# Routing from centred raw tokens in the mixtures of a macaron kernel

## The reference

```
x = x + 0.5 * ffn(layernorm(x))          # F0: two layers of local attention and gated MLP
x = x + ssm(layernorm(x))                # S
x = x + 0.5 * ffn(layernorm(x))          # F1
x = x + 0.5 * mixture(layernorm(x))      # M0
x = x + unit(layernorm(x))               # U: RMS norm, two projections, silu, product, output
x = x + 0.5 * mixture(layernorm(x))      # M1

def mixture(x):                          # 8 experts, top 2, hidden 512
    probs = softmax(x @ w_router)
    topk_w, topk_idx = top_k(probs, 2)   # weights are not renormalised over the two
    out_e = gelu(x @ w1[e] + b1[e]) @ w2[e] + b2[e]
    return sum over the chosen e of topk_w * out_e
```

## Time and profile before

| | us |
|---|---|
| median of 3 runs | 1197.33 (1192.86 to 1198.54) |
| profiled execution | 1189.11, span 1187.3 |
| PE busy | 1012.3 (85%) |
| DVE busy | 720.2 (61%) |
| ACT busy | 688.2 (58%) |
| POOL busy | 524.8 (44%) |
| mean granted TensorE clock | 0.926 |

### The profile page before, as it was taken

The page is one execution under the profiler, slowest core; times in us unless marked ns, Lnnn a source line. Parts: engine busy times, 40 slices in busy tenths (PEclk is TensorE's granted clock), DMA queues, the critical chain, the costliest instruction groups (busy, mean ns, idle before and its releaser), DMA issues.

```text
span 1187.3 us, 25908 instructions
## 1 busy us (share of the span) xinstructions
PE 1012.3 (85%) x9070; PEld 632.4 (53%) x9070; DVE 720.2 (61%) x1625; ACT 688.2 (58%) x1301; POOL 524.8 (44%) x405
## 2 busy tenths in 40 slices
PE   4788999999998876799999999999639968746995
PEld 1345555555555364355555555555339964325995
DVE  0577678777776653677776776876564423654441
ACT  2566686686673662676677667656316636623661
POOL 2664456556441542545444344433345530263451
PEclk9899999999999967999999999999759989857997
DMA  9895344455433600545444344432312240011223
GB/s 349 250 298 157 86 102 109 97 120 116 100 93 81 71 1 2 126 109 121 96 107 96 89 107 109 101 80 77 143 44 68 67 114 1 19 43 48 64 65 120
DMA packets 88511, 120.02 MB, mean 101 GB/s; under 512 B 20064, under 2 KB 72032, under 8 KB 87488
## 3 DMA queue, kind: packets, MB, share of 16 engines
q1 hardware_dynamic: 81824, 96.30, 33.8%
q0 software_dynamic: 6272, 20.44, 4.7%
q10 hardware_dynamic: 288, 1.63, 0.3%
HBM read 62.66 MB, written 22.11 MB: 71 GB/s over the span
## 4 chain that ended last, share of the span: by engine, by line
PE 65%; ACT 14%; issue 7%; DMA 6%; DVE 5%; POOL 1%; SPq 1%; ACTq 0%; DVEq 0%; POOLq 0%
PE banks L591 7%; PE banks L944 6%; PE banks L954 6%; PE banks L676 5%; PE banks L662 5%; PE banks L620 3%; PE banks L751 3%; PE banks L669 3%; PE banks L637 3%; PE banks L721 3%; PE banks L726 2%; PE banks L645 2%; DMA rstd<-arena 2%; ACT arena L1194 2%; ACT arena L1189 2%
## 5 line engine op out<-in xcount | busy, mean ns | idle before, releaser
L2041 POOL TENSOR_TENSOR arena<-arena 128x1024 f32<-128x1024 f32 x64 | 150.9, 2357 | 321.0 <-DVE arena L1644 318.7
L2030 POOL TENSOR_TENSOR arena<-arena 128x1024 f32<-128x1024 f32 x64 | 150.8, 2357 | 41.6 <-ACT arena L1189 41.6
L1636 DVE TENSOR_REDUCE arena<-banks 128x4 f32<-128x512 f32 x128 | 82.5, 686 | 93.5 <-PE banks L620 93.3
L1181 ACT ACTIVATE arena<-banks,arena 128x512 f32<-128x512 f32 x128 | 80.5, 679 | 93.6 <-PE banks L669 93.2
L591 PE MATMUL banks<-arena 128*128 128x512 f32 x256 | 128.6, 627 | 6.7 <-DVE arena L1563 5.9
L2020 POOL DMA_INDIRECT moe_outs<-arena x78 | 81.5, 1045 | 100.7 <-DVE arena L1882 88.6
L1386 ACT ACTIVATE arena<-banks,arena 128x128 f32<-128x128 f32 x312 | 89.0, 369 | 59.0 <-PE banks L944 58.9
L2013 POOL DMA_INDIRECT moe_rows<-arena x64 | 63.1, 986 | 118.5 <-DVE arena L1617 101.1
L1644 DVE TENSOR_TENSOR arena<-arena 128x1024 f32<-128x1024 f32 x64 | 78.1, 1220 | 28.4 <-DMA arena<-arena 28.4
L1194 ACT ACTIVATE arena<-banks 128x1024 f32<-128x1024 f32 x64 | 65.6, 1025 | 46.1 <-PE banks L591 45.1
L954 PE MATMUL banks<-arena 128*128 x624 | 87.5, 283 | 4.6 <-ACT arena L1386 4.4
(11 more groups left out here) (221 smaller groups left out, 1951.6 us busy)
## 6 DMA issues: line engine op xcount, KB each, us to landing
arena<-arena SPq DMA_DIRECT2D x256, 128.0 KB, 3.8
arena<-rstd SPq DMA_DIRECT2D x128, 256.0 KB, 4.3
moe_rows<-arena POOLq DMA_DIRECT2D x12, 903.0 KB, 6.6
arena<-moe_rows SPq DMA_DIRECT2D x78, 64.5 KB
arena<-in_rot SPq DMA_DIRECT2D x4, 1024.0 KB, 11.6
arena<-in_mw SPq DMA_DIRECT2D x2, 2048.0 KB, 10.8
arena<-moe_outs SPq DMA_DIRECT2D x16, 256.0 KB, 4.9
arena<-ssm_a SPq DMA_DIRECT2D x4, 512.0 KB, 6.6
```

The costliest lines, as they stand in the source:

```text
L1636: nc.vector.tensor_reduce(mx[:, e], by_row(bank[3 + e][:]), AX.X, ALU.max).then_inc(s_max, 1)
L2030: nc.gpsimd.tensor_tensor(TA[:, n % 2], RAW, ROTV[:, :, 0, c * C:(c + 1) * C], ALU.mult).then_inc(cos_done, 1)
L2041: nc.gpsimd.tensor_tensor(TA[:, n % 2], TA[:, n % 2], TB, ALU.add).then_inc(rot_sum, 1)
```

## The change

The mixture's norm no longer works on features as partitions. At the start of F1 the router matrix is multiplied with `centre` once (`centred_router`), and logits are raw: X times the centred router. VectorE picks the top two from these raw logits (`pick`, 5 steps, reading the accumulator). Tokens come out centred and transposed by one matmul with `centre` on the right (`token_rows`). VectorE takes the variance of each token with bn_stats and bn_aggr (`moments`), ScalarE makes the inverse roots, four columns a chunk, and scales the tokens while it copies them. The softmax weights (`gates_start`, `gates_exp`, `gates_end`) are computed once for all 16 tiles, behind the tile map. `rank` and the scatter are as before. In F1's tail chunks 1 and 2 are handled earlier; in the unit, `down(0)` and `added(0)` come before chunk 3 of M0 is combined, and each chunk of M1 enters by one step `enter`.

```diff
-        MX_CEN, MX_VAR = [(0, 3, 7, 3), (7, 7, 7, 7)], [(1, 4, 6, 5), (3, 4, 5, 3)]
+        MX_TOK, MX_RANK = [(0, 3, 3, 7), (7, 7, 3, 7)], [(1, 4, 4, 6), (3, 4, 5, 4)]
 # SP: ins["mwr"] -> WR is loaded behind WM[1] at the start, no longer at M0
 # TensorE
+            def centred_router():
+                pe.wait_ge(wrc, 16)
+                mm(bank[7][:, 0:NE], centre, WR, start=True, stop=True).then_inc(wrc, 1)
+            def route(moe, c):
+                pe.wait_ge(wrc, 18)
+                for t in range(TILES):
+                    at = c * C + t * P
+                    last = mm(bank[MX_RANK[moe][c]][:, t * NE:(t + 1) * NE], X[:, at:at + P], WRC, start=True, stop=True)
+                last.then_inc(router_mm, 1)
+            def token_rows(moe, c):
+                for t in range(TILES):
+                    at = c * C + t * P
+                    last = mm(bank[MX_TOK[moe][c]][:, t * P:(t + 1) * P], X[:, at:at + P], centre, start=True, stop=True)
+                last.then_inc(xtok_mm, 1)
 # TensorE, ffn tail (run 1): token_rows(0, 0) for centred, route(0, 0) for variance; then
-                    pe.wait_ge(xtok_done, 2)
+                    pe.wait_ge(xtok_done, 1)
                 transpose_out(30, n - 2, s, 0)
                 for e in range(2):
                     values(31, n - 1, e)
                 if run:
                     pe.wait_ge(x_ffn, NCH + 2)
-                    centred(X, 1, MX_CEN[0][1])
+                    token_rows(0, 1)
+                    route(0, 1)
...
                 last_variance()
                 if run:
-                    variance(mix, 1, MX_VAR[0][1])
+                    rank(0, 1)
                 mlp_output(6, s)
                 last_hidden(0)
                 last_hidden(1)
-                if run:
-                    route(mix, 0, 1)
                 last_hidden(2)
+                if run:
+                    pe.wait_ge(xtok_done, 3)
+                    pe.wait_ge(rank_dve, 2 * RANK_STEPS)
+                    pe.wait_ge(x_ffn, NCH + 3)
+                    token_rows(0, 2)
+                    route(0, 2)
                 mlp_output(7, s)
 # TensorE, start of mixture 0: rank(0, 2); token_rows(0, 3); route(0, 3); rank(0, 3)
 # TensorE, unit, order after: mixed(2) up(0) centred(2) down(0) mixed(3) up(1) enter(0) variance(2)
 #   centred(3) down(1) rank(0) variance(3) enter(1) up(2, 0..2) rank(1) up(2, 3) up(3)
 #   down(2) down(3) enter(2) rank(2) enter(3) rank(3)
+                def enter(c):
+                    pe.wait_ge(x_unit, c + 1)
+                    if c == 2:
+                        pe.wait_ge(rank_dve, RANK_STEPS * (NCH + 1))
+                    elif c:
+                        pe.wait_ge(xtok_done, 2 * NCH + (1 if c == 1 else 3))
+                    token_rows(1, c)
+                    if c in (1, 2):
+                        pe.wait_ge(sn_out, SN0 + c + 2)
+                    elif c == 3:
+                        pe.wait_ge(rank_dve, RANK_STEPS * (NCH + 2))
+                    route(1, c)
 # ScalarE
             def tokens(moe, c):
+                act.wait_ge(tok_dve, 2 * k + 2)
+                A(RSTD[:, tt], MOMENT[:, tt, 1], ACT.Ln, bias=eps_c).then_inc(tok_act, 1)
+                act.wait_ge(tok_act, 2 * k + 1)
+                A(RSTD[:, tt], RSTD[:, tt], ACT.Exp, scale=-0.5, bias=zero_c).then_inc(tok_act, 1)
+                act.wait_ge(tok_act, 2 * k + 2)
                 act.wait_ge(xtok_mm, k + 1)
...
+                for t in range(TILES):
+                    at = c * TILES + t
+                    last = A(XTOK[:, 0, at, 0:DM], bank[MX_TOK[moe][c]][:, t * P:(t + 1) * P], ACT.Copy, scale=RSTD[:, at:at + 1])
+                last.then_inc(xtok_done, 1)
+                act.wait_ge(xtok_done, 2 * k + 1)
+                A(XTOK[:, 1, tt, 0:DM], XTOK[:, 0, tt, 0:DM], ACT.Copy).then_inc(xtok_done, 1)
 # ScalarE, ffn tail: tokens(0, 1) where norm_root(1) was, tokens(0, 2) where tokens(0, 1) was
 # ScalarE, unit: tokens(1, 0) behind square(3), tokens(1, 1) behind logs(3), 2 and 3 behind the silus
 # VectorE
+            def pick(moe, c):
+                dve.wait_ge(router_mm, k + 1)
+                for t in range(TILES):
+                    last = nc.vector.max(TOPL[:, c * TILES + t], part(moe, c, 0)[:, t])
+                chained(last, pick_dve)
 # then max_index, copy to float, one-hot marks and their sum as before
+            def moments(moe, c):
+                dve.wait_ge(xtok_mm, k + 1)
+                for t in range(TILES):
+                    last = nc.vector.bn_stats(PART[:, c * TILES + t], bank[MX_TOK[moe][c]][:, t * P:(t + 1) * P])
+                last.then_inc(tok_dve, 1)
+                dve.wait_ge(tok_dve, 2 * k + 1)
+                for t in range(TILES):
+                    last = nc.vector.bn_aggr(MOMENT[:, c * TILES + t], PART[:, c * TILES + t])
+                last.then_inc(tok_dve, 1)
 # VectorE, ffn tail, order after: normalise(31) maximum subtract moments(0, 0) divide(30) pick(0, 0)
 #   divide(31) gate(6, 0) rank(0, 0) residual(7) pick(0, 1) gate(6, 1) moments(0, 1) gate(6, 2)
 #   mlp_norm(7) rank(0, 1) mlp_residual(6) gate(7, 0..2) pick(0, 2) moments(0, 2) mlp_residual(7)
 # VectorE, mixture 0: rank(0, 2) pick(0, 3) moments(0, 3) rank(0, 3), then in both mixtures
 #   tile_map() gates_start() weights of two tiles gates_end() diagonals
 # VectorE, unit, order after: scaled(1) gates(0) added(0) update(3) gates(1) moments(0) pick(0)
 #   log_ratio(2) normed(2) rank(0) added(1) scaled(2) log_ratio(3) normed(3) moments(1) pick(1)
 #   scaled(3) rank(1) gates(2) gates(3) added(2) added(3) pick(2) moments(2) rank(2) pick(3) moments(3) rank(3)
```

More of the change, by code:

```diff
@@ L224, in macaron_kernel @@
         top[0] = rot0
-        MB1, MB2, WR = cols(NE * MB), cols(NE * DM), cols(NE)
+        MB1, MB2 = cols(NE * MB), cols(NE * DM)
         by_tile = lambda n: cols(T // P * n).rearrange("p (t e) -> p t e", e=n)
-        PB, MINE, TOPV, IDXF = [by_tile(NE) for _ in range(4)]
+        PB, MINE, TOPL, IDXF, GATE = [by_tile(NE) for _ in range(5)]
+        PART, MOMENT = by_tile(6), by_tile(2)
+        RSTD = cols(T // P)
         PRE = cols((T // P + 1) * NE).rearrange("p (t e) -> p t e", e=NE)
@@ L296, in macaron_kernel @@
             "rms_act", "xn_done", "uv_mm", "uv_silu", "gated", "uo_mm", "unit_sum")]
-        ln_cen, ln_sq, ln_var, ln_log, ln_rstd, ln_mid, ln_out = [sem("ln_" + n) for n in (
-            "cen", "sq", "var", "log", "rstd", "mid", "out")]
+        ln_cen, ln_sq, ln_var, ln_log, ln_rstd, ln_out = [sem("ln_" + n) for n in (
+            "cen", "sq", "var", "log", "rstd", "out")]
         mlp_out, yb_ready = sem("mlp_out"), sem("yb_ready")
@@ L1075, in _ @@
                 if kind == "F":
+                    if run:
+                        centred_router()
                     first_centred(norm0, 0, run)
@@ L1289, in ffn @@
                 evacuate_out(31, n - 1, 0)
-                if run:
-                    norm_square(mix, 1, MX_CEN[0][1])
-                else:
+                if not run:
                     ssm_square(0, 0)
@@ L1310, in ffn @@
                 if run:
-                    tokens(0, 1)
+                    tokens(0, 2)
                 else:
@@ L1590, in route @@
-                for t in range(c * TILES, (c + 1) * TILES):
-                    last = nc.vector.max(TOPV[:, t], PB[:, t])
-                chained(last, route_dve)
-                for t in range(c * TILES, (c + 1) * TILES):
-                    last = nc.vector.max_index(TOPI[:, t], TOPV[:, t], PB[:, t])
-                chained(last, route_dve)
-                chained(nc.vector.tensor_copy(IDXF[:, tt], TOPI[:, tt]), route_dve)
-                each = expert_id.unsqueeze(1).unsqueeze(1).to_broadcast([P, TILES, 2, NE])
@@ L1750, in ffn @@
                 normalise(31, n - 1)
-                if run:
-                    norm_chunks(mix, first_plain, [0])
                 maximum(n - 1)
                 subtract(n - 1)
+                if run:
+                    dve.wait_ge(cos_done, n)
+                    moments(0, 0)
                 divide(n - 2)
                 if run:
-                    dve.wait_ge(cos_done, n)
-                    route(0, 0)
+                    pick(0, 0)
                 divide(n - 1)
@@ L1763, in ffn @@
                 residual(7, gg - 1)
+                if run:
+                    pick(0, 1)
                 gate(6, gg - 2, 1)
+                if run:
+                    moments(0, 1)
                 gate(6, gg - 2, 2)
                 mlp_norm(7, gg - 1)
+                if run:
+                    rank(0, 1)
                 mlp_residual(6, gg - 2)
-                if run:
-                    norm_chunks(mix, first_plain, [1])
-                else:
+                if not run:
                     ssm_normed(0, 0)
@@ L1775, in ffn @@
                 if run:
-                    route(0, 1)
+                    pick(0, 2)
+                    moments(0, 2)
                 else:
```

(9 more changed lines are left out.)

196 lines of the change are left out of this document (74 added, 122 removed).

## The result

The changed kernel took 1174.11 us in the median of four runs (1171.05 to 1180.05), the kernel before 1196.62 (four runs, 1192.86 to 1198.54): a ratio of 0.9836, 95% interval 0.9809 to 0.9863; that is 19.6 us of 1196.62, and the two medians stand 22.5 apart. The forecast was 1179 in 1169 to 1190. On the chip of the first set of experiments the same kernel gave 0.9834 [0.9775, 0.9894], in the third 0.978 [0.9748, 0.9812].

The account below looks back on a forecast made before the run. GpSimd's indirect writes, 32 a stage at 1.272 us each, were taken to bound the ways into both expert stages. Gains 8.5 + 11.3 - 1.6 = 18.2 us off the median 1197.33 gave 1179 us, range 1169 to 1190.

Parts of the forecast that it names:

- Moments: VectorE's bn_stats and bn_aggr for one chunk: 1.35 us, bounds 0.75 to 2.4.
- token step: ScalarE's inverse roots and scaled copies of one chunk's tokens: 2.45 us, bounds 2.0 to 3.5.
- First mixture: Way into the first expert stage: chunk 2's writes start at 848.1, their pace ends at 868.4, gain 8.5 us.
- The diagonals: VectorE's products beside the last three or four writes of each stage: 0.8 us lost each, from nothing to 1.6.
- Second mixture: Way into the second expert stage: chunks 2 and 3 written without gap from 1042.7 to 1063.05, gain 11.3 us.
- The cover at the end: First mixture's end: VectorE's tail work done at 868.7, first expert rows about 872.7, so 4 us of cover.
- only one stage gains: Rival: new work before the output projection grows in the ffn's tail and eats the first gain; 1188 us, chance 0.11.
- nothing arrives: Rival: chunk 2's ranking chain isn't shortened because TensorE's order there waits elsewhere; 1197 us, chance 0.08.
- all writes run without a gap: Rival: GpSimd writes gap-free from chunk 0 in both stages, gains 13.5 and 20.8; 1163 us, chance 0.05.
- The rival with VectorE's hold: VectorE's two-operand products stop GpSimd's write building; the diagonals cost 4.9 us a round, not 0.8; 1187 us, chance 0.12.
- The forecast's sign: GpSimd's writes beside the diagonals were to take 1.0 to 1.4 us.
- The rival with slow moments: VectorE's bn_stats and bn_aggr pairs slow: gain gone from 1.5 us a pair, 1207 us at 2.1; chance 0.06.

Follow-up runs that it names:

- first set: Changed kernel again and three variants (router matrix loaded late, F1's tail or unit's first chunk in old order) on one chip; kernel before 1184.7 us, variants 1166.73 to 1174.94.
- after: Profiled execution of the changed kernel from the first measurement, against the kernel before; 1180.05 us, its slowest run.
- control of the first set: Changed kernel once more, no edit, against the kernel before on the first set's chip: 1166.71 us, ratio 0.9834.
- both controls: Changed kernel run again without edit in the first and third sets, against the kernel before: 1166.71 us (0.9834) and 1170.06 us (0.978).
- third set: Changed kernel again, late diagonals, early ranking added, then moments first added, on another chip than the first set; 1170.06, 1170.84, 1171.4, 1172.8 us; kernel before 1194.74.

## Why the prediction was right

**The new operations.** Moments were taken at 1.35 and are 1.30 (0.88 + 0.04 + 0.38); the token step at 2.45 and is 2.47 (819.67 to 822.14); token rows at 0.95, are 1.05 for eight passes. The output projection, forecast for 820.2, is at 827.09 - 6.83 = 820.26. The bounds came from neighbours of the same kind, a reduction of 128 columns and a quartet of activations with a per-token scale; both values came out where the forecast took them, a little below the middle, but two cases don't make a rule.

**First mixture.** Chunk 0 was put at 822.8 and came at 822.6, chunk 1 at 835.2 and came at 835.35, chunk 2 at 848.1 and came at 849.4 in this trace, 848.35 in the first set. The gap ahead of chunk 2 is 4.13 us and not 2.7. TensorE, then VectorE, in after:

```profile
846.33 0.96 PE L572 MATMUL banks<-arena 128*128 128x8 f32 x8
```

```profile
847.89 0.39 DVE L1562 MAX8 arena<-banks 128x8 f32<-128x8 f32 x4 [1.34 <-PE banks L572]
...
852.20 0.76 DVE L1695 SCALAR_TENSOR_TENSOR arena<-banks,arena 64x512 f32<-64x512 f32 x1 [0.55 <-issue]
```

The sum had VectorE wait for these logits as well. They end at 847.29 - 6.83 = 840.46 where it had 840.05. The rest of the miss is two stops that it didn't have: 0.60 us between the end of the logits and the pick, and 0.55 inside chunk 3's residual. In the control of the first set the pick starts 0.04 us after the logits and the second stop is absent. The diagonals, taken at 0.8, cost 0.8 here (1.20 + 1.50 - 2 x 0.97) and 1.3 in both controls, where the last three writes are all long. Of that, 0.45 us stood in the kernel before already (its last write of 1.42), so the loss against it is 0.3 to 0.85. By the marks the stage gave 7.4 us in the first set, 6.7 in this trace and 6.1 in the third set, where 8.5 - 0.8 = 7.7 was said.

**Second mixture.** Chunk 2's writes were put at 1042.7 and came at 1045.18 - 4.75 = 1040.4, in the two controls 1.1 and 2.6 later than that; the stage gave 11.3 to its second tile in the first set, 12.6 in this trace and 9.8 in the third set, where 11.3 - 0.8 = 10.5 was said. Inside it errors cancelled, and that the sum came out so near is luck in part. The silu table is 0.7 late (1.1 said), but the first four silus then run back to back and the sum of chunk 2 ends 3 us sooner than forecast. From the sum to the first write it takes 9.0 us where 8.3 were said: TensorE starts the token rows 0.49 us after the sum, and VectorE the pick 0.78 after the logits. VectorE adds chunk 3 before it picks, which the sum had left out, but that ends at 1038.34 and the logits at 1038.51, so it costs nothing.

**The cover at the end** held: from the start of the last write to the second tile's matmul it is 6.8 us before, 6.9 in after.

**The other rivals.** That only one stage gains is refuted by 7.4 and 11.3; that nothing arrives, by chunk 2's start, which moved from 55.8 to between 47.5 and 48.6 us; that all writes run without a gap, by the 4.13 and 5.63 us ahead of chunk 2.

**The rival with VectorE's hold** was right in kind and wrong in size. Eight products of 0.61 us lie beside three writes and lengthen each by at most 0.53, 1.3 us in all and not 4.9. The forecast's sign, writes of 1.0 to 1.4 us, was a little low for 1.13 to 1.51. Not every write beside them is longer: with the moments taken twice the last write of the first mixture starts 0.5 us after the products and takes 0.99. Before, the tile map's 0.48 us products beside the writes added nothing:

```profile
868.33 0.48 DVE L1843 TENSOR_TENSOR arena<-arena 128x312 f32<-128x312 f32 x1
```

```profile
868.08 0.97 POOL L2013 DMA_INDIRECT moe_rows<-arena  x1 [0.30 <-issue]
```

By the Trainium skill, "SBUF — State Buffer", section "SBUF: two separate sides", a VectorE operation with two SBUF inputs and a GpSimd operation that reads SBUF take a shared port pair as an exclusive lock, and the one that comes second is fully blocked for the whole instruction. The trace agrees that there is a hold. It also shows the writes going on between the products, none held for longer than one of them (0.53 against 0.61 us). That this lock is what holds them is not shown.

**Slips in the sum.** The upper bounds of the costs leave a gain of 18.2 - 4.2 - 5.3 - 1.6 = 7.1 us and not 8, the lower ones 24.6 and not 24; that leaves the range as it is. The rival with slow moments counted eight rounds before chunk 2's rank in each chain, while the bounds counted three chunks, twelve, in the first mixture; the kernel with the moments taken twice shows three.

**From 18.2 to 20.** The measured 1174.11 us is 4.9 under the forecast of 1179. The ratios give 19.6 us (first measurement), 19.7 (first set) and 26 (third), the marks 19.3, 18.7 and 15.9. The rest isn't in the two stretches. Three things of this size vary from run to run where the code is equal: the start (first rotation sum at 33.98 to 39.08 over the profiles of the changed kernel and its variants), the time from the first rotation sum to the last (762.8 to 768.6 us, 766.9 in the profile of before), and the expert stages, 87.1 to 94.3 us for the first and 90.1 to 95.7 for the second over the ten profiles of the changed kernel's tile loop. The profile of before is 1189.11 us where that kernel's median was 1197.33, so it can't say what its slower runs spend, and what the 0.3 to 10 us above the marks are stays open.

## What to carry to other kernels

When a row of equal writes at a fixed pace ends a stage, find the last gap in it: what closes that gap moves the end, and a hold put ahead of it and behind it shows in two runs which side a chunk is on. Mind what other engines do beside the last writes: it changed their length by up to 1.3 us a stage. Moving work to shorten a chain counts only down to the next thing in wait: here early ranking took 2.2 us out and a wait of 2.6 us stood in its place. The new norm, with one matmul and per-token moments, gained nothing in the first mixture in the old order; with the new order the stage gave 7.4 us. In the second mixture 10 us stay when chunk 0 goes back to its old place. Here the cheaper steps paid only where the order let the next chunk use them.

## What the runs showed of the hardware that was not expected

Chunk 2's start in the first mixture goes with the chip: 47.5 us in the three kernels of the first set with this order, 48.6 to 49.4 in the four of the other chip that don't touch its chain. Two stops of VectorE make the difference between the controls, 0.57 us more between the logits and the pick, and 0.47 ahead of chunk 3's residual; with two chips, that the chip is the cause isn't shown. In the same part of VectorE's program stand the stops of 1.50 and 2.31 us with the moments first, and of 2.60 and 3.49 us, after a matmul that TensorE had finished, in both kernels that rank early. No releaser is known for any of them, and no run took them apart: part of what is left to win in the first mixture lies there. Expert tiles sometimes stop for their rows: the chain of waits of after has

```profile
896.07 3.52 DMA arena<-moe_rows
...
935.51 3.54 DMA arena<-moe_rows
```

and that of the control in the first set has no such step, with its expert stage 7.2 us shorter. It can't be all of the spread, since the kernel with the router loaded late has no such step either and a stage of 93.4 us. Why the loads are late in one run and not in another was not tried.
